# Block sums of two small-head attentions inverted by way of DRAM, and turned maxima copied by ScalarE

## What is computed

```python
q = q * cos + _rotate_half(q) * sin
k = k * cos + _rotate_half(k) * sin
scores = jnp.einsum('bhqd,bhkd->bhqk', q, k) * scale       # S = 2048 keys, H = 16, D = 8
attn = jax.nn.softmax(scores, axis=-1)
out = jnp.einsum('bhqk,bhkd->bqhd', attn, v)
...
scores = jnp.where(causal, scores, jnp.float32(-1e+30))    # the second one
p = jax.nn.softmax(scores, axis=-1)
```

## Time and profile before

| | us |
|---|---|
| median of 3 runs | 2145.32 |
| lowest and highest | 2144.81, 2145.73 |
| span of the profiled execution | 2143.6 |
| busy: TensorE matmul | 1853.8 |
| busy: VectorE | 1599.2 |
| busy: ScalarE | 1374.3 |
| busy: GpSimd | 314.9 |

### The profile page before, as it was taken

How to read it: one execution, slowest core, us unless ns; L and a number is a source line. 1 busy time by engine, 2 the same in 40 slices (tenths; PEclk the granted TensorE clock), 3 DMA queues, 4 the chain that set the end, 5 groups by cost and what they waited for, 6 DMA issues and landing times. The chain is left out here.

```text
span 2143.6 us, 40610 instructions
## 1 busy us (share of the span) xinstructions
PE 1853.8 (86%) x16064; PEld 920.6 (43%) x16064; DVE 1599.2 (75%) x2327; ACT 1374.3 (64%) x2546; POOL 314.9 (15%) x464
## 2 busy tenths in 40 slices
PE   6799999989999669849989999999668998998585
PEld 2122222222222249824766776777412332334385
DVE  6899999999995343445777777877588989786324
ACT  3489989989888433434555556566246987877331
POOL 2000000000000160432431221211110000000123
PEclk7589999999999869968999999999888999999788
DMA  5000000000000149600000000000100000000084
GB/s 163 1 4 4 7 5 4 7 4 5 5 4 7 43 146 309 230 17 1 1 1 1 1 1 1 1 1 1 51 1 2 7 5 7 7 7 11 12 281 155
DMA packets 51356, 81.36 MB, mean 38 GB/s; under 512 B 7520, under 2 KB 36192, under 8 KB 51040
## 3 DMA queue, kind: packets, MB, share of 16 engines
q1 hardware_dynamic: 46000, 70.30, 10.4%
q0 software_dynamic: 3072, 6.30, 0.9%
q10 hardware_dynamic: 2096, 2.17, 0.4%
HBM read 62.49 MB, written 11.67 MB: 35 GB/s over the span
## 5 line engine op out<-in xcount | busy, mean ns | idle before, releaser
L633 DVE TENSOR_REDUCE a_mx<-psum 128x2 f32<-128x1024 f32 (+2 forms) x832 | 908.8, 1153 | 70.6 <-PE psum L434 45.5
L567 ACT ACTIVATE a_cs<-psum 128x512 f32<-128x512 f32 (+3 forms) x1664 | 858.3, 572 | 125.8 <-PE psum L454 79.5
L479 PE MATMUL psum<-a_cs,a_V 128*16 128x256 f32 (+1 forms) x6400 | 505.9, 387 | 12.0 <-ACT a_OD L544 9.5
L434 PE MATMUL psum<-a_KS,a_QS 48*128 48x512 bf16 (+3 forms) x1664 | 326.1, 386 | 61.2 <-DVE a_mx L633 59.4
L454 PE MATMUL psum<-a_QS,a_KS 51*128 51x512 bf16 (+3 forms) x1664 | 337.6, 381 | 6.9 <-ACT a_cs L567 3.8
L1767 PE MATMUL psum<-b_VW,b_ST 128*128 128x129 f32 x2176 | 251.6, 277 | 13.0 <-DVE X L1877 13.0
L1767 PEld LDWEIGHTS psum<-b_VW,b_ST 128*128 128x128 f32 x2176 | 247.5, 193 | 14.7 <-DVE X L1877 14.7
L454 PEld LDWEIGHTS psum<-a_QS,a_KS 51*128 51x128 bf16 x1664 | 87.2, 93 | 364.4 <-ACT a_cs L567 320.7
L1748 PE MATMUL psum<-b_GT,AT 128*128 128x512 f32 (+3 forms) x640 | 242.0, 532 | 1.6 <-ACT b_ST L1803 1.6
L479 PEld LDWEIGHTS psum<-a_cs,a_V 128*16 128x16 f32 x6400 | 107.5, 94 | 261.7 <-issue 125.5
L1852 DVE TENSOR_TENSOR b_M<-b_M,b_ST 128x512 f32<-128x512 f32 (+3 forms) x288 | 174.9, 607 | 41.9 <-ACT b_ST L1803 12.1
(11 more groups left out here) (213 smaller groups left out, 1533.5 us busy)
## 6 DMA issues: line engine op xcount, KB each, us to landing
e_W<-in_l_experts SPq DMA_DIRECT2D x46, 576.0 KB, 5.2
e_W<-in_l_experts SPq DMA_DIRECT2D x22, 768.0 KB, 4.9
yg<-e_yout SPq DMA_DIRECT2D x14, 256.0 KB, 5.9
xg<-zeros SPq DMA_DIRECT2D x2, 1472.0 KB, 9.5
a_cs<-in_rope ACTq DMA_DIRECT2D x4, 512.0 KB, 8.8
a_QS<-a_mrow SPq DMA_DIRECT2D x128, 3.0 KB
a_num<-a_OD SPq DMA_DIRECT2D x128, 16.0 KB
a_den<-a_OD SPq DMA_DIRECT2D x128, 16.0 KB
```

The lines of the kernel that those rows point to most:

```text
L434: mm = pe.matmul(ps[:, 2 * slot + half, 0:width], QS[rows, 2 * p + i, q_cols(qb, qt * P, P)], KS[rows, 2 * p + i, c * BLK:c * BLK + width] ...
L479: mm = pe.matmul(ps[32 * j:32 * j + 2 * HD, AV_BANK, a:b], V[:, kt, HPP * p + j, :], probs(e, a, b), start=(kt == 0 and half == 0), stop=last,
L567: act.activation(probs(e, c, BLK), ps[:, S_BANK + e % S_SLOTS, c:BLK], ACT.Exp, scale=scale).then_inc(exp_done, 1)
L633: dve.tensor_reduce(mx[:, pk % 2, qt, 2 * i:2 * i + 2, c], banks, AX.X, ALU.max).then_inc(max_done, 1)
```

## The change

For all but the last block of each attention the sums go another way. The gather sends one row of sums a head to a DRAM tensor `sums` instead of 8 equal rows to `a_den`. When a block's gathers have landed, SyncE reads them back as 128x64 into `a_denc` (`spread_sums`), VectorE takes the reciprocal of 128x64 (`invert`, one step earlier: `FINISH` = 5), SyncE writes it to a DRAM tensor `inverse`, waits for that, and reads it back in 16 DMAs, one a head, each row spread over 8 partitions, into `a_rden` (`spread_inverse`). GpSimd does the product, placed in its stream behind the split of the second pack of the next block; for the third block of the causal attention, behind the split of the last pack. `finished` is now counted by GpSimd, and the gathers of the next block wait for it as before.

The turned maxima of every pack but the first now take a bank of the exponentials' ring of three instead of a slot of the maxima's ring, and ScalarE copies them to `a_mrow`, after the exponentials of the same half step.

```diff
-FINISH = 6
+FINISH = 5
...
+        self.entries = []
+        for u, row in enumerate(self.halves):
+            self.entries += [("exp", HPP * (u // 2) + 2 * (u % 2) + half) for half in range(2)]
+            self.entries += [item for item in row if item[0] == "turn"]
+        self.place_of = {entry: n for n, entry in enumerate(self.entries)}
+
+    def bank(self, entry):
+        return S_BANK + self.place_of[entry] % S_SLOTS
...
+        def wait_bank(eng, entry):
+
+            n = plan.place_of[entry]
+            if n < S_SLOTS:
+                return
+            what, of = plan.entries[n - S_SLOTS]
+            if what == "exp":
+                eng.wait_ge(exp_done, of + 1)
+            else:
+                wait_row(eng, of)
...
                         h = (HPP * p + j) * HD
-                        for dst, r in ((num, 32 * j), (den, 32 * j + HD)):
-                            sp.dma_start(dst[h:h + HD, :], OD[r:r + HD, p, :]).then_inc(gathered[p], 16)
+                        sp.dma_start(num[h:h + HD, :], OD[32 * j:32 * j + HD, p, :]).then_inc(gathered[p], 16)
+                        r = 32 * j + HD
+                        if k < NB - 1:
+                            row = k * HEADS + HPP * p + j
+                            sp.dma_start(sums[row:row + 1, :], OD[r:r + 1, p, :]).then_inc(gathered[p], 16)
+                        else:
+                            sp.dma_start(den[h:h + HD, :], OD[r:r + HD, p, :]).then_inc(gathered[p], 16)
+
+                def spread_sums(k):
+
+                    for p in range(NPACK):
+                        sp.wait_ge(gathered[p], 16 * 2 * HPP * (k + 1))
+                    if k:
+                        sp.wait_ge(inverse_ready, k)
+                    sp.dma_start(denc[:, :], sums[k * HEADS:(k + 1) * HEADS, :].rearrange("h (c q) -> (h c) q", c=HD)).then_inc(sums_in, 16)
+
+                def spread_inverse(k):
+
+                    mine = inverse[k * HEADS:(k + 1) * HEADS, :]
+                    sp.wait_ge(inverse_ready, k + 1)
+                    sp.dma_start(mine.rearrange("h (c q) -> (h c) q", c=HD), rdenc[:, :]).then_inc(inverse_out, 16)
+                    sp.wait_ge(inverse_out, 16 * (k + 1))
+                    if k:
+                        sp.wait_ge(finished, k)
+                    for h in range(HEADS):
+                        sp.dma_start(rden[h * HD:(h + 1) * HD, :],
+                                     mine[h:h + 1, :].broadcast_to([HD, BLK])).then_inc(inverse_in, 16)
 
                 todo = [(plan.due[pk][0], 0, pk) for pk in range(NPK)]
                 todo += [(plan.first[pk + 1] + 1.5, 1, pk) for pk in range(NPK)]
-                for _, what, pk in sorted(todo):
-                    (shift, gather)[what](pk)
+                todo += [(plan.first[NPACK * (k + 1)] + 2, 2, k) for k in range(NB - 1)]
+                todo += [(plan.first[NPACK * (k + 1)] + FINISH + 0.2, 3, k) for k in range(NB - 1)]
+                for _, what, n in sorted(todo):
+                    (shift, gather, spread_sums, spread_inverse)[what](n)
...
+                    for k in range(NB - 1):
+                        if pk == (NPK - 1 if causal and k == NB - 2 else NPACK * (k + 1) + 1):
+                            for p in range(NPACK):
+                                pool.wait_ge(gathered[p], 16 * 2 * HPP * (k + 1))
+                            pool.wait_ge(inverse_in, 16 * HEADS * (k + 1))
+                            pool.tensor_tensor(OT[:, q_cols(order[k], 0, BLK)], num[:, :], rden[:, :], ALU.mult).then_inc(finished, 1)
...
                 def max_item(item):
+                    if item in plan.place_of:
+                        wait_bank(pe, item)
+                        turn(item[1], plan.bank(item)).then_inc(s_ready, 1)
+                        return
...
+                def row_copy(pk):
+                    entry = ("turn", pk)
+                    act.wait_ge(s_ready, plan.place_of[entry] + 1)
+                    if pk >= 2:
+                        wait_shift(act, pk - 2)
+                    act.activation(mrow[:, pk % 2, :], ps[0:TR, plan.bank(entry), :], ACT.Copy).then_inc(row_ready, 1)
+
                 for s in range(NS):
...
+                    for half in range(2):
+                        for j in (2 * half, 2 * half + 1):
+                            exponential(s, j)
+                        for item in plan.halves[2 * s + half]:
+                            if item[0] == "turn":
+                                row_copy(item[1])
...
-                def finish(k):
+                def invert(k):
+                    dve.wait_ge(sums_in, 16 * (k + 1))
+                    if k:
+                        dve.wait_ge(inverse_out, 16 * k)
+                    dve.reciprocal(rdenc[:, :], denc[:, :]).then_inc(inverse_ready, 1)
```

More of the change, by code:

```diff
@@ L156, in __init__ @@
             count += item[0] == "scores"
+        self.halves = []
+        for row in self.rows:
+            cut = (len(row) + 1) // 2
+            self.halves += [row[:cut], row[cut:]]
+        self.entries = []
[5 more added lines that the diff above has]
+        return S_BANK + self.place_of[entry] % S_SLOTS
     def lay(self, ahead):
@@ L251, in small_head_stage @@
         mrow = sb("mrow", [TR, 2, BLK], BF16)
+        denc, rdenc = sb("denc", [P, BLK // HD]), sb("rdenc", [P, BLK // HD])
+        sums, inverse = (nc.dram_tensor(f"{tag}_{n}", ((NB - 1) * HEADS, BLK), F32, kind="Internal").ap()
+                         for n in ("sums", "inverse"))
         tokens_in = sem("tokens_in")
@@ L412, in mask, with turn @@
                                 mm.then_inc(ready, 1)
+                def turn(pk, bank):
+                    if opening and pk == 0:
+                        pe.wait_ge(opening.cast, 4)
+                    pe.wait_ge(split_done, pk + 1)
+                    for qt in range(TPB):
+                        mm = pe.matmul(ps[0:TR, bank, qt * P:(qt + 1) * P],
+                                       mterm[:, pk % 2, qt, :, :].rearrange("p h t -> p (h t)"),
+                                       core.identb[:, :], start=True, stop=True)
+                    return mm
                 def max_item(item):
+                    if item in plan.place_of:
+                        wait_bank(pe, item)
+                        turn(item[1], plan.bank(item)).then_inc(s_ready, 1)
+                        return
                     slot = slot_of(item)
                     if item[0] == "turn":
[L417 to L425, removed]
+                        turn(item[1], 2 * slot).then_inc(max_ready, 1)
                         return
@@ L449, in score @@
                     for half in range(2):
-                        e = e0 + half
-                        if e >= S_SLOTS:
-                            pe.wait_ge(exp_done, e - S_SLOTS + 1)
+                        entry = ("exp", e0 + half)
+                        wait_bank(pe, entry)
                         rows = slice(HALF * half, HALF * half + ROWS)
-                        mm = pe.matmul(ps[:, S_BANK + e % S_SLOTS, c:BLK], KS[rows, 2 * p + i, kt * P:(kt + 1) * P],
+                        mm = pe.matmul(ps[:, plan.bank(entry), c:BLK], KS[rows, 2 * p + i, kt * P:(kt + 1) * P],
                                        QS[rows, 2 * p + i, q_cols(qb, c, BLK - c)], start=True, stop=not diagonal,
@@ L459, in score @@
                     if diagonal:
-                        mask([S_BANK + (e0 + half) % S_SLOTS for half in range(2)], slice(c, c + P), core.neg2t,
+                        mask([plan.bank(("exp", e0 + half)) for half in range(2)], slice(c, c + P), core.neg2t,
                              s_ready, True)
@@ L508, in _ @@
                 for s in range(NS):
-                    row = plan.rows[s]
                     for half in range(2):
                         score(s, half)
-                        for item in row[half * (len(row) + 1) // 2:len(row) if half else (len(row) + 1) // 2]:
+                        for item in plan.halves[2 * s + half]:
                             max_item(item)
```

53 lines of the change are left out of this document (31 added, 22 removed).

## The result

The changed kernel takes 2128.2 us (median of four runs, 2125.6 to 2132.0) where the kernel before takes 2145.5 beside it: ratio 0.9923, interval 0.9909 to 0.9938. It is faster by 0.8%. I had predicted 2150.1 us, with a range of 2139 to 2156. The prediction was wrong in its sign.

What follows compares the result with a forecast made beforehand. VectorE's row maxima were taken to set the first attention's pace, the second being bound more evenly. Terms -14.9 + 2.1 + 1.3 + 5.6 + 10.7 = +4.8 us, onto the median 2145.3: 2150.1 us, range 2139 to 2156.

Steps and rivals of the forecast that it cites:

- The one unknown that weighs: Issue time of a row read from DRAM into 8 partitions, in no profile row; taken as 0.67 us.
- Rival (a): Cheap reads: 0.47 us an issue, each of three chains 3.1 us shorter, total 2140.8 us; chance 15%.
- First attention, the finish: Three finishes leave VectorE for three reciprocals of an eighth of the size: -14.9 us, with 1.6 us margin.
- First attention, the turned maxima: Copies moved to ScalarE gain nothing; the second score matmul waits for an exponential, 0.15 us a pack: +2.1 us.
- Rival (c): In the first attention the copy taken off VectorE counts: -9.4 instead of +2.1, total 2138.6 us; chance 10%.
- Second attention, the turned maxima: Only 0.5 us, at the end, for two row copies that ScalarE does ahead of output copies.
- Second attention, block 0: TensorE waits 5.0 us for pack 5's shift rows, queued behind the 16 reads; the finish's 4.9 are spent: +1.3 us.
- Rival (d): Nobody waits in the second attention's blocks 0 and 1: -4.9 and -5.2 us, total 2133 us; chance 5%.
- Block 1: Second attention: TensorE stands at pack 10's turn for GpSimd's split, queued behind the product: +5.6 us.
- Block 2 and the end: Second attention: the finish, hidden before, becomes a SyncE chain ahead of the last 32 gathers: +10.7 us.
- Rival (b): Slow landings in DRAM: one more us for each write, total 2155 us; chance 20%.

Runs made afterwards that it cites:

- sources: Changed kernel with the 16 reads' source differing by block (one DRAM row, eight DRAM rows, eight SBUF rows; result wrong): second attention 350.79 us, no ratio.
- sums_only: Changed kernel with the turned maxima left on VectorE in the maxima's banks, sums by way of DRAM: ratio 0.9916 to the kernel before.
- turns_only: Kernel before with only the turned maxima moved to the exponentials' banks and ScalarE, every finish still on VectorE: ratio 0.9986 to the kernel before.
- one_read: Changed kernel with one DMA of 128 rows in place of the 16 reads: second attention 338.33 us, ratio 0.9905 to the kernel before.
- reads_twice: Changed kernel with 16 more reads to a spare tile ahead of each run of 16: second attention 362.76 us, ratio 1.0002 to the kernel before.

## Why the prediction was wrong, point by point

**The failed step is "The one unknown that weighs".** I gave a read of 8 partitions from DRAM 0.67 us, the price of the 8-row copies inside SBUF, with 0.47 as its lowest bound. It takes 0.34. What the copies share with the reads is the row count, and that isn't what costs; "sources" has both row counts from DRAM at 0.34 and the copy inside SBUF at 0.67. The bound could have been seen. The trace of before has the loads of the experts' weights, from DRAM too (line 1053), and shift rows, which are 3 rows inside SBUF and no cheaper than 8 (line 306; duration ns, min/median/max):

```profile
L1053 SPq DMA_DIRECT2D e_W<-in_l_experts x68: 337/338/3400, 763.5 to 2104.6; - x68
```

```profile
L306 SPq DMA_DIRECT2D a_QS<-a_mrow x128: 639/641/885, 93.9 to 1980.3; - x128
```

I had bounded the price by one load of 0.43 us and not looked for the cheapest issue with a source in DRAM. Rival (a) had the right mechanism and too high a price. With 0.34 in the prediction's own working each chain is 16 x 0.33 = 5.3 us shorter. Block 0's wait of 5.0 us is gone, so it gains the 4.9 of the finish; block 1 comes to 5.6 - 5.3 = +0.3, the end to 10.7 - 5.3 = +5.4. The second attention is then +0.8 (measured +0.95), and the forecast 2145.3 - 14.9 + 2.1 + 0.8 = 2133 us.

The rule that I had weighed (the Trainium skill, DMA: Bandwidth & Descriptors, section "Why a DMA increments its semaphore by 16 and not by 1") tells how many engines a copy uses and that the sequencer writes the missing counts. I read out of it that 8 rows are dear wherever they come from, and it does not say that: it puts no time on those counts. Nor do the traces bear my reading out: 8 rows from DRAM are issued in 0.34 us, in both forms.

**First attention, the finish: -14.9.** Right. The three packs are 4.9 us shorter each, -14.7 with their turns in it. `sums_only`, without the turns, has 37.44 us against 42.48, 3 x 5.04 = 15.1. The margin held, and the low clock around each finish is gone with the pause.

**First attention, the turned maxima: +2.1.** The mechanism was right (VectorE idle for 0.62 us instead of copying, the second score matmul behind the exponential), the size a little under: 0.12 us a pack. Rival (c), that the copy counts, is refuted by "sums_only" and "turns_only". What I had not seen is 2.3 us at the last turn, which go with the clock; they stand in the last section.

**Second attention, the turned maxima.** I put them at nothing but 0.5 us at the end. `sums_only` has them at 1.7 us, 0.75 of it in packs 0 to 3 and 0.9 in block 0.

**Second attention, block 0: +1.3, measured -4.1.** Wrong by the price; with it put back, +1.7. Rival (d), "nobody waits", came true here for a reason that it did not name. Its -5.2 for block 1 was too much even so: with the wait gone (`one_read`) the block is 3.9 us shorter than before.

**Block 1: +5.6, measured +0.2.** The wait of TensorE for a split queued behind GpSimd's product was right in place and cause: 3.02 us, 8.65 with the price put back, 0.31 with the product moved.

**Block 2 and the end: +10.7, measured +4.4.** The price is most of the difference (5.3 by its own working, 5.6 by `reads_twice`). The DRAM landings were priced too long as well: the sums' last write to the read 1.5 us (taken 2.5), the read to the reciprocal 1.7 (2.1), the inverse's write to the reads 1.6 (2.5). Rival (b), slow landings, lost. The sentence that I had set beside it (the Trainium skill, DMA: Bandwidth & Descriptors, section "Anatomy of one DMA — SWDGE (gpsimd) path", HBM as the heaviest target) is about GpSimd's path, and no row here bears it out for SyncE's: at 32 KB a write to DRAM lands in 1.5 us, faster than the 2.5 of the 256 KB store in the earlier trace rows. Late shift rows ate part of that: the inverse was ready at 1956.98 + 0.55 = 1957.53, and its write stood behind them until 1960.32. The last of the 32 gathers is issued 20.9 us after the first (20.8 taken).

**The rest, -2.5 us**, lies in stages that the change doesn't touch, and is less than they differ between two traces of one kernel's code. It can't be given a cause.

So of the 22 us between forecast and result, 16.6 are in the second attention, and "reads_twice" gives 17.0 of them back by the price alone; 3.0 are in the first attention, most of it clock, and 2.5 elsewhere. The range failed too: its lower end rested on a bound that was none.

## What to carry to other kernels

Price a new DMA by the rows that share its source and target memories, not by those that share its shape, and take as its lower bound the cheapest issue of that kind in the whole trace. Where one such price is multiplied by 16 in each of three chains, a factor of two is worth the whole gain; one DMA with a repeated row in its pattern removes the multiplication, and a second queue shortens a tail of eight copies (7.5 us to 5.7 here). Work moved off an engine that waits at that place anyway gains nothing; it can cost something where it lands, and more once the waits that hid it are gone.

## What the runs showed of the hardware that I had not expected

**Issue times on a queue** by where the bytes are: SBUF to SBUF, 8 rows of 2 KB, 0.62 us (0.67 from issue to issue), on SyncE's queue whether ScalarE's is issuing or not, and on ScalarE's 0.63 to 0.70 (but for one issue of 1.46); 3 rows of 1 KB inside SBUF, 0.64; DRAM to SBUF, 8 rows, 0.30 us (0.34), whether one row is repeated or eight are read; SBUF to DRAM, 0.42 us for one row and 0.46 for eight. A read of 256 KB in one DMA, each row repeated eight times, is issued in 0.62 us and landed in 3.4.

**The same pause, three clocks.** At the last turn of the first attention TensorE stands still for 2.55 us in every one of the traced kernels. TensorE at that turn, before, with the sums only, and changed:

```profile
672.25 0.48 PE L422 MATMUL psum<-identb,a_mterm 128*12 128x128 bf16 x3 [2.56 <-POOL a_mterm L353]
```

```profile
655.61 0.33 PE L485 MATMUL psum<-identb,a_mterm 128*12 128x128 bf16 x3 [2.55 <-POOL a_mterm L413]
```

```profile
659.21 0.33 PE L489 MATMUL psum<-identb,a_mterm 128*12 128x128 bf16 x3 [2.55 <-POOL a_mterm L417]
```

And the window of the 7 us behind it in the three kernels (the granted clock is the number behind the brackets of the last engine):

```profile
672.00:679.00 7.00, 6.75 (x52) 1.55 (x52) 0.68 (x1) 3.45 (x7) 0.11 (x1) 0.53 0.01 2
```

```profile
655.60:662.60 7.00, 6.89 (x62) 1.69 (x62) 0.68 (x1) 4.79 (x10) 0.00 (x0) 0.76 0.01 2
```

```profile
659.20:666.20 7.00, 6.79 (x73) 2.04 (x73) 0.00 (x0) 6.30 (x13) 0.00 (x0) 1.00 0.01 2
```

The clock granted behind the same pause is the lower level (1.2 GHz) nearly throughout, for half of the time, or not at all, and the pack takes 39.9, 38.7 and 37.7 us. The value repeats wherever the first attention has the same order (37.6 to 37.7 in all eight others that have the changed kernel's; 38.7 in the two others with the sums by way of DRAM and the turns on VectorE), so it isn't noise. `turns_only`, with the old finishes, is near the kernel before: 39.7 us, at a granted clock of 0.56. So about half of the 2.3 us goes with the sums and half with the turns on top of them. That the clock makes the difference is read from the three windows, and no run changes it alone; why the same pause is answered in three ways, none shows. These 2.3 us are a part of the gain that no accounting of operations would have found.
